# A two-layer graph network: 128-node message tiles, one attention row in four added by VectorE, three products moved

## The reference, cut to what matters

```python
messages = (h[src] + e) @ msg_W + msg_b                    # e = edge_emb[edge_type]
att_in = concat([h[src], h[dst], e, task])
delta = tanh(gelu(att_in @ att_W1 + att_b1) @ att_W2 + att_b2)
weight = 1 + edge_scale * delta
agg = segment_sum(messages * weight, dst) / max(segment_sum(weight, dst), 1)
y = h + gelu(concat([h, agg]) @ up_W1 + up_b1) @ up_W2 + up_b2
out = x + layernorm(y)
```

## Time and profile before

| | |
|---|---|
| median of three runs | 1305.84 us |
| the profiled execution | 1307.77 us, its span 1305.8 us |
| PE busy | 937.8 us (72%) |
| DVE (VectorE) busy | 899.9 us (69%) |
| POOL busy | 831.5 us (64%) |
| ACT (ScalarE) busy | 605.0 us (46%) |
| mean granted clock of TensorE | 0.798 of full speed |

### The profile page before, as it was taken

How to read it: one execution, slowest core, us unless ns; L and a number is a source line. 1 busy time by engine, 2 the same in 40 slices (tenths; PEclk the granted TensorE clock), 3 DMA queues, 4 the chain that set the end, 5 groups by cost and what they waited for, 6 DMA issues and landing times. The chain is left out here.

```text
span 1305.8 us, 18685 instructions
## 1 busy us (share of the span) xinstructions
PE 937.8 (72%) x5019; PEld 728.9 (56%) x5019; DVE 899.9 (69%) x2594; ACT 605.0 (46%) x1479; POOL 831.5 (64%) x868
## 2 busy tenths in 40 slices
PE   7505455664123511389899999999999999999985
PEld 6402233332112510277677777777777777777774
DVE  6477575665566544345656888888888888888658
ACT  6433333433243433223325665566666656556544
POOL 0377777777777777663127777777777777777012
PEclk9855555555555555589899999999999999999988
DMA  5568666566776666544357777877877787887312
GB/s 157 133 201 279 220 214 216 201 224 221 241 261 232 201 204 216 191 116 130 69 152 231 235 234 235 241 235 234 238 239 236 232 236 241 234 235 237 99 38 85
DMA packets 100774, 263.58 MB, mean 202 GB/s; under 512 B 21094, under 2 KB 42117, under 8 KB 94530
## 3 DMA queue, kind: packets, MB, share of 16 engines
q0 software_dynamic: 53856, 164.87, 42.7%
q1 hardware_dynamic: 45026, 95.76, 22.1%
q10 hardware_dynamic: 1792, 1.75, 0.5%
HBM read 192.92 MB, written 68.25 MB: 200 GB/s over the span
## 5 line engine op out<-in xcount | busy, mean ns | idle before, releaser
L675 POOL DMA_INDIRECT gath<-hp_d,chain_src x391 | 370.8, 948 | 169.3 <-issue 166.3
L1353 POOL DMA_INDIRECT gbuf<-pm_d,srcs x350 | 332.1, 949 | 108.5 <-issue 104.1
L922 DVE SCALAR_TENSOR_TENSOR hist<-hist,smask,ps 128x256 f32<-128x256 f32 x390 | 186.7, 479 | 194.8 <-ACT ps L716 186.8
L716 ACT ACTIVATE ps<-gath,chain_w 128x256 f32<-128x256 f32 x391 | 164.6, 464 | 312.9 <-DMA gath<-hp_d,chain_src 295.1
L1750 DVE TENSOR_TENSOR acc<-ps,acc 112x272 f32 x418 | 183.7, 439 | 69.2 <-DVE acc L1750 64.0
L1596 ACT ACTIVATE ps<-ps 128x512 f32<-128x512 f32 x210 | 122.1, 582 | 191.7 <-PE ps L1492 191.6
L1492 PE MATMUL ps<-gbuf,ident 128*128 128x256 f32 x700 | 210.1, 382 | 0.0
L1490 PE MATMUL ps<-qw,halves 128*128 x1254 | 206.6, 274 | 2.3 <-DVE qw L1699 2.3
L1516 PE MATMUL ps<-gbuf,placed 128*112 128x272 f32 x700 | 175.4, 393 | 1.0 <-ACT placed L1615 0.7
L837 PE MATMUL ps<-win_hot,node_hot 128*112 128x28 bf16 x391 | 43.7, 253 | 175.2 <-DVE win_hot L1009 175.2
L1490 PEld LDWEIGHTS ps<-qw,halves 128*128 128x128 bf16 x1254 | 122.9, 98 | 73.8 <-issue 6.9
(11 more groups left out here) (292 smaller groups left out, 1384.2 us busy)
## 6 DMA issues: line engine op xcount, KB each, us to landing
hist_d<-hist SPq DMA_DIRECT2D x48, 1024.0 KB, 4.6
gath<-hp_d,chain_src POOLq DMA_INDIRECT x391, 3.1
wn<-node_row_d SPq DMA_DIRECT2D x26, 224.0 KB
key<-node_row_d SPq DMA_DIRECT2D x26, 224.0 KB, 3.5
gbuf<-pm_d,srcs POOLq DMA_INDIRECT x350, 4.0
pm_d<-gbuf SPq DMA_DIRECT2D x6, 896.0 KB, 5.1
hb_d<-gbuf SPq DMA_DIRECT2D x7, 448.0 KB, 3.2
qw<-hb_d SPq DMA_DIRECT2D x7, 448.0 KB, 8.4
```

Source lines behind the costliest of these rows:

```text
L675: eng.indirect_dma_start(row_at(j), None, hp_d[:, :], bass.IndirectOffsetOnAxis(ap=chain_src[:, j:j + 1], axis=0)).then_inc(got[q % RINGG] ...
L716: eng.activation(weighted_at(j), row_at(j), ACT.Copy, scale=chain_w[:, j:j + 1]).then_inc(gw_ready, 1)
L922: eng.scalar_tensor_tensor(out=state_at(j), in0=state_at(j - 1) if j else first_state[:, :], scalar=smask[:, j:j + 1], in1=weighted_at(j), ...
L1353: eng.indirect_dma_start(gath3(g % RING)[:, k, 0:2 * D], None, pm_d[:, :], bass.IndirectOffsetOnAxis(ap=srcs[:, g * SG + k:g * SG + k + 1] ...
```

## The change

The message tiles no longer follow the windows: `up` now holds the two halves of the transposed rows one behind the other for all nodes (`nodes`), and a tile is 128 nodes (`tiles_of`). There are 25 tiles, in groups of 3, 4, 3, 4, 3, 4 and 4 (the last tile has 64 nodes). The copy to `up` becomes two instructions. QE goes from 3 to 1: Q of groups 1 and 2 is made behind the messages. `own_early` is gone: all 14 pairs are made in the edge stage, at every seventh group from the 6th. In the edge stage TensorE leaves out the identity product of the fourth slot of each full group (104 of the 105); VectorE adds the gathered rows in PSUM instead, behind `match_keys`, and ScalarE's second gelu waits for it (`p_added`). In the last stage VectorE's `update(1)` stands before `rows_y(0)`.

```diff
-            U0, US, UE = 6, 11, 5
+            U0, US = 6, 7
+            def nodes(n0, n1, half):
+                return up[:, half * NT * WIN + n0:half * NT * WIN + n1]
+            def tiles_of(i):
+                first, last = i * GN * WIN // P, (i + 1) * GN * WIN // P
+                return range(first, last if i < NG - 1 else -(-NM // P))
+            def p_by_vector(g, k):
+                return slots_in(g) == SG and k == SG - 1
-            QE = 3
+            QE = 1
...
-                def messages(i, ks):
+                def messages(i):
                     eng.wait_ge(hT_ready, i + 1)
-                    for k in ks:
+                    for k, m in enumerate(tiles_of(i)):
...
-                                ins = eng.matmul(bank(4 + k)[0:WIN, half * D:(half + 1) * D], up[:, at + hf * WIN:at + (hf + 1) * WIN],
+                                ins = eng.matmul(bank(4 + k)[0:n, half * D:(half + 1) * D], nodes(m * P, m * P + n, hf),
...
                 for i in range(QE, NG):
                     keys_q(i)
-                    if i == QE + 1:
-                        own_early(0)
-                for p in range(1, UE):
-                    own_early(p)
                 eng.wait_ge(q_low, NG)
+                eng.wait_ge(pm_a, by_act(NG))
+                eng.wait_ge(pm_v, by_vec(NG))
...
                             for part in range(3):
-                                eng.matmul(to, hot[g % 2][:, k * P:(k + 1) * P],
-                                           qw[:, bass.ds(w[k] * (3 * D) + part * D, D)], start=part == 0, stop=False)
-                            ins = eng.matmul(to, ident[:, :], gath3(r)[:, k, 0:D], start=False, stop=True)
+                                ins = eng.matmul(to, hot[g % 2][:, k * P:(k + 1) * P],
+                                           qw[:, bass.ds(w[k] * (3 * D) + part * D, D)], start=part == 0,
+                                           stop=part == 2 and p_by_vector(g, k))
+                            if not p_by_vector(g, k):
+                                ins = eng.matmul(to, ident[:, :], gath3(r)[:, k, 0:D], start=False, stop=True)
...
@@ scalar, edge_step
                             eng.wait_ge(z_ready, g * 2 + half + 1)
+                            if half == 1 and slots_in(g) == SG:
+                                eng.wait_ge(p_added, g + 1)
...
@@ vector, message loop
-                    eng.tensor_copy(up[:, i * GN * ACW0:(i + 1) * GN * ACW0].rearrange("p (k c) -> p k c", k=GN),
-                                    bank(4, 2).rearrange("p (k c) -> p k c", k=GN)[:, :, 0:ACW0]).then_inc(hT_ready, 1)
+                    for hf in range(2):
+                        ins = eng.tensor_copy(nodes(i * GN * WIN, (i + 1) * GN * WIN, hf).rearrange("p (k n) -> p k n", k=GN),
+                                              bank(4, 2).rearrange("p (k c) -> p k c", k=GN)[:, :, hf * WIN:(hf + 1) * WIN])
+                    ins.then_inc(hT_ready, 1)
...
@@ vector, edge_step
                     if has(g + 1):
                         match_keys(g + 1)
+                    if has(g) and slots_in(g) == SG:
+                        eng.wait_ge(z_ready, g * 2 + 2)
+                        zk = bank(2 * (g % 2), 2)[:, (SG - 1) * D:SG * D]
+                        eng.tensor_tensor(zk, zk, gath3(r)[:, SG - 1, 0:D], ALU.add).then_inc(p_added, 1)
...
                 update(0)
+                update(1)
                 rows_y(0)
                 shifts(0)
-                update(1)
```

More of the change, by code:

```diff
@@ L1162, in gnn_two_layers @@
             gath = [gbuf[:, r * SG * SW:(r + 1) * SG * SW] for r in range(RING - 1)] + [attw[:, :]]
-            pm = [gbuf[0:WIN, r * GN * 2 * D:(r + 1) * GN * 2 * D] for r in range(2)]
+            pm = [gbuf[:, r * GN * 2 * D:(r + 1) * GN * 2 * D] for r in range(2)]
             h, hb, ngb = ([gbuf[0:WIN, (4 + 2 * n + r) * GN * D:(5 + 2 * n + r) * GN * D] for r in range(2)] for n in range(3))
@@ L1216, in gnn_two_layers @@
             z_ready = sem("z_ready")
+            p_added = sem("p_added")
             gelu_ready = sem("gelu_ready")
@@ L1229, in gnn_two_layers, with pair_cols, nodes_in, by_act @@
             block = b34.enter_context(nc.Block())
-            U0, US, UE = 6, 11, 5
-            assert U0 + US * (NT // 2 - UE - 1) + 1 < NGR
+            U0, US = 6, 7
+            assert U0 + US * (NT // 2 - 1) + 1 < NGR
             def pair_of(g):
[L1235 to L1241, removed]
+                return (g - U0) // US if g >= U0 and (g - U0) % US == 0 and (g - U0) // US < NT // 2 else None
+            def nodes(n0, n1, half):
+                return up[:, half * NT * WIN + n0:half * NT * WIN + n1]
+            def pair_cols(p, half):
+                return nodes(p * 2 * WIN, (p + 1) * 2 * WIN, half).rearrange("p (k n) -> p k n", k=2)
+            NM = NT * WIN
+            def tiles_of(i):
+                first, last = i * GN * WIN // P, (i + 1) * GN * WIN // P
+                return range(first, last if i < NG - 1 else -(-NM // P))
+            def nodes_in(m):
+                return min(P, NM - m * P)
+            def by_act(i):
+                return sum((len(tiles_of(n)) + 1) // 2 for n in range(i))
+            def by_vec(i):
+                return sum(len(tiles_of(n)) // 2 for n in range(i))
             def slots_in(g):
                 return min(SG, USED - g * SG)
+            def p_by_vector(g, k):
+                return slots_in(g) == SG and k == SG - 1
             def gath3(r):
@@ L1266, in pm_parts @@
             def pm_parts(i):
-                return [(0, GN)] if i < NG - 1 else [(0, 2), (2, 3), (3, 4)]
+                return [(0, len(tiles_of(i)))] if i < NG - 1 else [(0, 2), (2, 3), (3, 4)]
+            assert len(tiles_of(NG - 1)) == GN and max(len(tiles_of(i)) for i in range(NG)) <= GN
             def put_all(eng):
@@ L1286, in _ @@
                     for k0, k1 in pm_parts(i):
[L1287 to L1291, removed]
+                        eng.wait_ge(pm_a, by_act(i) + (k1 + 1) // 2)
+                        eng.wait_ge(pm_v, by_vec(i) + k1 // 2)
+                        m0, m1 = tiles_of(i)[k0], tiles_of(i)[k1 - 1] + 1
+                        n = nodes_in(m1 - 1)
+                        eng.dma_start(pm_d[m0 * P:(m1 - 1) * P + n, :].rearrange("(k p) d -> p k d", p=n),
+                                      rows_by_k(pm[i % 2])[0:n, k0:k1, :]).then_inc(pm_out[i % 2], 16)
                     if i == REC_AT:
@@ L1452, in _ @@
                         turn_n(i + 2)
-                    messages(i, range(GN))
+                    messages(i)
                     if i + 2 < NG:
@@ L1660, in take @@
                         eng.wait_ge(pm_out[i % 2], 16 * (i // 2))
-                    eng.wait_ge(pm_ready, GN * i + k + 1)
-                    eng.tensor_copy(pm[i % 2][:, k * 2 * D:(k + 1) * 2 * D], bank(4 + k)[0:WIN, :]).then_inc(pm_v, 1)
+                    if k >= len(tiles_of(i)):
+                        return
+                    m = tiles_of(i)[k]
+                    n = nodes_in(m)
+                    eng.wait_ge(pm_ready, m + 1)
+                    eng.tensor_copy(pm[i % 2][0:n, k * 2 * D:(k + 1) * 2 * D], bank(4 + k)[0:n, :]).then_inc(pm_v, 1)
                 def biases(i):
```

60 lines of the change are left out of this document (19 added, 41 removed).

## The result

The changed kernel takes **1327.6 us** (median of four runs, 1327.27 to 1329.13), the kernel before 1305.73 (1302.63 to 1306.84): 1.7% slower, ratio 1.0174, 95% interval 1.0155 to 1.0193. The forecast was 1314.5 us: right in its sign and inside its range, but the loss is 22 us where 9 were forecast.

A forecast was written before the change was run, and what follows sets the result against it. VectorE was taken to bound the edge stage: start -12.0 + 0.3, addition +28.9, last stage -8.5 make +8.7 us on the profiled 1307.8, 1316.5, or 1314.5 us as median; range 1308 to 1328.

The forecast's parts named there:

- What bounds the edge stage: Edge stage: VectorE's group of 4.94 us has no room for more work; PE 4.88 without a pair, POOL 5.0.
- the wait for gelu: Edge stage: VectorE's third dot product waits for ScalarE's second gelu behind the addition, 0.03 us more per group.
- The room of 8.5 us: Edge stage: VectorE alone needs 498.9 of 507.4 us, so 8.5 us is real waiting, given back against the addition.
- The start of the edge stage: Up to the edge stage: messages end 19.5 us earlier, six Q give back 7.5, so it starts 12.0 us earlier.
- the half-clock stretch: Message loop: the late copy and PE's half-clock products behind it go away, -4.2 us.
- The last stage: Last stage: the second update ahead of `rows_y(0)` on VectorE ends PE's wait for it, -8.5 us.
- The conversion to the median: Whole kernel: 1.9 us taken off, as the profiled execution before lay that far above the median of the runs.
- Pairs at no cost: Edge stage: five more pairs on PE, 8 us, fit its idle time; they cost 8 us if VectorE isn't the bound.
- A: Edge stage: VectorE's gaps are slack and take up the addition, -2.4 us there, 1283 us in all; chance 10%.
- B: Whole kernel: Q's chain runs at PE's pace, the addition costs +24.8 without gelu's wait, sides cancel, 1305 us; 14%.
- C: Edge stage: first bank's gelu is late too, the round over ScalarE is exposed, 0.3 us per group, 1345 us; 6%.
- D: Edge stage: PE's idling lets its clock fall to half, one fall in ten groups adding 36 us, 1350 us; 5%.

The follow-up runs named there:

- e8: Kernel before plus one fp32 addition of 256 columns per group on VectorE, into scratch, that nobody waits for: 1332.28 us, ratio 1.0207.
- e6: Kernel before with VectorE's accumulations, now of group g - 2, placed between the dot products of group g: 1302.78 us, ratio 0.9992.
- e2: Changed kernel with VectorE's addition moved ahead of `match_keys`: 1316.50 us, ratio to before 1.0105.
- e3: Kernel before with only VectorE's `update(1)` called ahead of `rows_y(0)`: 1298.32 us, ratio 0.9939.
- e4: Kernel before with only VectorE's addition of the fourth P rows; tiles, Q, pairs and last stage as before: 1343.99 us, ratio 1.0306.
- e5: Changed kernel with VectorE's accumulations, now of group g - 2, placed between the dot products of group g: 1277.38 us, ratio to before 0.9806.
- e7: Changed kernel with VectorE's addition only in the 14 groups with a pair, on TensorE elsewhere: 1287.86 us, ratio to before 0.9889.
- e1: Changed kernel with the addition undone (fourth slot's product on TensorE again), the rest kept: 1293.31 us, ratio to before 0.9906.
- e12: The kernel of e5 run again on another chip, where every kernel took 17 to 20% longer: 1530.8 us, ratio to before 0.9949.

## Why the prediction was right in its direction and wrong in its size

- **What bounds the edge stage: right as far as it decides.** VectorE's own group lasts 4.94 us and its gaps can't take an addition that stands behind them (e8). PE needs 4.88 us and with its pairs 5.02 on average, POOL 5.0; which of these two held the kernel before is not told apart (e6). The change takes 0.43 us from PE and gives 0.33 to one that has no room.
- **The step that failed: the wait for gelu.** It was put at 0.03 us, from two hand-overs of 0.03. The rows have 0.115: gelu starts 0.10 us behind the addition's end, and not 0.03, so the third dot product starts 0.46 us behind the second instead of 0.345. 0.085 us more in 101 groups are 8.6 us, and e2, which takes away this wait alone, gets 10 us back in the stage. This is most of the miss. The 0.03 was read behind a PE product (0.03 or 0.04 from the end of its row, an end that the profile models) and carried over to VectorE without a row of that pair of engines; the 0.03 from gelu to the dot product held (0.03 or 0.04 in all groups). The argument that a dot product of another bank covers the addition was right only for its length, not for the way over ScalarE and back: 0.42 + 0.10 + 0.58 + 0.03 = 1.13 us against 1.02.
- **The room of 8.5 us: too large by 2.5.** The waits that the addition was to fill held some accumulations that start 1.0 us behind the one before instead of 0.65, and late starts behind the last dot product. Four and three such are there after the change too (1.4 and about 0.6 us in all). They are not waits for PE. The edge stage grew by 39.4 us: 33.8 for the addition (101 x 0.334, forecast 34.3), 11.6 for gelu (3.0), less 6.0 (8.5).
- **The start of the edge stage: nearly right, in part by luck.** 11.3 us earlier by z, 10.9 by the first accumulation; 12.0 and 11.7 were forecast. The six Q take 689.35 - 657.87 = 31.5 us (31.4), with the residues 5.5, 3.6, 4.7, 3.6 and 4.7 us apart, as laid out. The messages end at 657.9 (657.3), but the loop got only 17.2 us shorter of the 19.5; 1.7 came from ahead of it, where traces of the same code differ by as much (the first tile stands at 575.5 to 577.2 in those of before, e3, e4, e6 and e8). The term that was too large is the half-clock stretch: one still stands in the loop, two groups earlier (i = 2 and not 4), behind the wait of 1.70 us at 602.96, where four products take 1.92 us. In e5 and e7, which share this loop, it is absent and the loop takes 80.7 us. So it comes and goes between executions, and is worth 1.7 us here.
- **The last stage: right.** -8.7 us; e3 gives -7.3 for it alone, whose interval holds it.
- **The conversion to the median** took 1.9 us off for the profiled run of before; the changed kernel's profiled run, 1327.44, lies at its median. So 1.9 of the 13 us is the spread of the runs, and 10.9 is the sum's: 10.5 in the edge stage, 0.8 at its start, -0.2 at the end.
- **The range held by luck.** For the edge stage alone its upper end allows 28.9 + 6.1 = 35.0 us, with 0.40 us for each addition; 39.4 came. The median lies inside 1308 to 1328 because that end also adds up losses that did not come (2 us at the start, 3 fewer gained ahead, 2.5 fewer at the end).
- **Pairs at no cost: right.** With VectorE as the bound they are free (e4 and the changed kernel have the same group). The prediction put them at 8 us if it were not; in e1, where PE has all its products again, the group is 5.10 instead of 5.03 us, which is 7 us.
- **Rivals.** A is refuted by e8. B failed on both of its sides: Q's chain took 31.5 us and not PE's pace, and the addition cost 39.4 in the stage and not 24.8. C is ScalarE's round too, but its condition, a late gelu of the first bank, did not come: the second dot product follows the first after 0.34; the second bank's gelu alone cost 0.115 where C had 0.3 more. D did not come in this kernel: PE idled about 8% of the stage at the full clock. In the disturbed e12 the clock was lower.

## What to carry to other kernels

An engine's share of busy time is not its room: measure the distance from one round to the next when it waits for nobody, its own semaphore waits included, and compare that between engines before moving work. Work handed to another engine costs its length and also the way that the result goes on; lay that way out row by row with the hand-over of that very pair of engines, and put other work of the receiver in between. Here the gaps behind dependent accumulations were the resource: with independent instructions in them, a change that loses 22 us became one that gains 27, of which the parts without the addition bring 12 by themselves (e1). Where VectorE was not what held the kernel back, the same filling brought nothing (e6).

## What the runs showed of the hardware

- Where ScalarE waited for VectorE's addition, gelu started 0.09 to 0.10 us after the addition's end; behind PE's products in the kernel before it was 0.03 to 0.04 after the end of the row, which is a modelled one.
- An fp32 addition of 256 columns takes VectorE 0.33 to 0.34 us from start to start with one input and the output in PSUM (after) and 0.33 with all in SBUF (e8): the same.
- Dependent accumulations stand 0.65 us apart (before), and 0.35 lies between such an accumulation and an independent instruction behind it (e5): of the 0.44 us that such a row shows, 0.08 overlapped the next one's start where that one didn't wait for it, and where it did, 0.21 was added.
